# Two layers of RWKV, attention and experts: the order of the splits in the expert loop

## The chip, the cores and the metric

One core of a Trainium2 chip runs the whole program in one launch. The metric is the device time of an execution, in microseconds (us). Three executions of the kernel before took 2056.88, 2056.96 and 2059.65 us; the median is 2056.96.

## What is computed

The input is 16 sequences of 256 tokens of width 256, so 4096 tokens. Four sublayers follow each other, each with its residual and a layer norm: an RWKV attention, a quantized feed-forward net, a latent attention with 16 heads, and a mixture of 32 experts with a shared expert. Only the last one is touched:

```python
C = int(math.ceil(CF * T / E))
...
Xp = x[slots_token].reshape(E, C, d)
G = jnp.einsum('ecd,edi->eci', Xp, W_gate)
U = jnp.einsum('ecd,edi->eci', Xp, W_up)
Y = jnp.einsum('eci,eid->ecd', jax.nn.silu(G) * U, W_down)
Yf = Y.reshape(EC, d) * slots_w[:, None]
out = jnp.zeros((T, d), x.dtype).at[slots_token].add(Yf)
shared = jax.nn.silu(x @ shared_gate.T) * (x @ shared_up.T) @ shared_down.T
return (out + shared).reshape(b, s, d)
```

Each of the 32 experts has 160 slots (tokens routed to it), an inner width of 128, and weights of 256x128, 256x128 and 128x256. The shared expert has an inner width of 256 and works on all tokens.

## The kernel before

The program is a chain of phases; the last is `moe_phase`, from line 2315. Earlier phases leave the tokens' rows in DRAM (`x3`), the rows of every expert's slots in DRAM (`slots`), and six of the sixteen units of 256 tokens with their shared part done. `moe_phase` does 32 experts and the shared part of the ten units that are left (`LATE`), seven of them (`INSIDE`) within the expert loop.

Every float32 product is made of three products of float32r parts. A value is split into a high part (ACT copies it with rounding) and a low part (DVE subtracts the high part from the value), and PE sums high by high, high by low and low by high. So each operand costs an operation on ACT, then one on DVE, before PE may use it.

One expert e goes through these steps:
- SP loads its weights (`load_w`, L2416, one DMA of 384 KB into a ring of seven raw buffers) and its slots' rows (`load_slots`, L2423, into a ring of eight).
- ACT and DVE split the weights: `weights_high(e)` L2533, 128x768, and `weights_low(e)` L2646. The parts lie in a ring of three (`WRING`).
- PE transposes the rows into one PSUM bank (`expert_turn`, L2799), ACT and DVE split them: `rows_high(e)` L2540, 128x320, and `rows_low(e)` L2651. The bank is single, so the turn of the next expert waits for `rows_low`.
- PE makes the gate and up products (`expert_in`, L2813, six matmuls each), for which it waits for `rows_low(e)` and `weights_low(e)`, and for the banks to be read.
- ACT applies silu (`expert_gate`, L2548), DVE multiplies (`expert_hidden`, L2660), ACT and DVE split the product (`hidden_high` L2554, `hidden_low` L2665).
- PE makes y (`expert_out`, L2824), which waits for `hidden_low(e)` and for the copy of the y before; ACT copies y with the slots' weights (`copy_y`, L2562, two operations).
- POOL adds the rows of y into one of two DRAM arrays (`add_rows`, L2475, two indirect DMAs with accumulation; expert e uses array e % 2). It waits for the copy and, since both write the same array, for the adds of expert e-2 to have landed.

SP's loads are tied to this: `load_w(e+7)` waits for `weights_low(e)`, and `load_slots(e+7)` waits for the turn and for the landed adds of expert e-1, as the same ring place is used by its index columns.

Each engine has its own order, written out by hand as a loop over e. `unit_of(e)` gives e // 4 and the piece e % 4: four experts go with one unit u of the shared part. In iteration e:
- PE (L2834): turn(e+2); in piece 0 the shared gate products, in piece 1 the shared up products; `expert_in(e+1)`; in piece 1 the turn of the next unit's tokens, in piece 2 the shared down products; `expert_out(e)`.
- ACT (L2574): `copy_y(e-1)`; in piece 2 `x_high(u+1)` L2512; `weights_high(e+2)`; `rows_high(e+2)`; `expert_gate(e+1)`; in piece 0 the shared gate L2519, in piece 1 the shared high part L2526; `hidden_high(e+1)`.
- DVE (L2676): in piece 0 `add_shared(u-1)` L2641, in piece 2 `shared_low(u)` L2635; `weights_low(e+2)`; in piece 1 `shared_hidden(u)` L2630; `rows_low(e+2)`; in piece 2 `x_low(u+1)` L2622; `expert_hidden(e+1)`; `hidden_low(e+1)`.

After the loop PE, ACT and DVE do the shared part of the last three units. SP waits for all adds and then loads the two arrays unit by unit (`load_sums`, L2453). DVE (`combine`, L2707 and L2711) and POOL (`add_first`, L2489) add them to the units' totals, and layer norm and the store of the result follow. On DVE `combine` of the first unit (p = 0) stands ahead of the last unit's `shared_hidden`.

Of the kernel before, what the change touches and what calls it, by code (L numbers as in the profile page):

```python
# [525 lines left out]
E = 32  # L526
# [1785 lines left out]
INSIDE = 7  # L2312


def moe_phase(nc, w_experts, x3, slots_dram, sums_dram, out, ident, q_rows, wq_high, raw_kept):
    with ExitStack() as ctx:
# [77 lines left out]
        def unit_of(e):  # L2394

            return e // PACE, e % PACE
# [110 lines left out]
        def _(act):  # L2507
            def x_high(u):
                act.wait_ge(transposed, u + 1)
                if u >= 2:  # L2510
                    act.wait_ge(up_ready, u - 1)
                nc.scalar.activation(xt_part[0][:, u % 2, :, :], xt_ps[:, :].rearrange("p (k t) -> p k t", k=KD),  # L2512
                                     ACT.Copy).then_inc(xt_high, 1)
# [14 lines left out]
            def weights_high(e):  # L2528
                if e >= EARLY_RAW:
                    act.wait_ge(raw_in[e % WRAW], 16 * (e // WRAW + (0 if e % WRAW < EARLY_RAW else 1)))  # L2530
                if e >= WRING:
                    act.wait_ge(y_ready, e - WRING + 1)
                nc.scalar.activation(w_part[0][:, e % WRING, :], kept_raw(q_rows, raw_kept, e), ACT.Copy)\  # L2533
                    .then_inc(w_high, 1)

            def rows_high(e):
                act.wait_ge(e_turned, e + 1)
                if e >= 2:
                    act.wait_ge(e_up_ready, e - 1)
                nc.scalar.activation(e_part[0][:, e % 2, :, :],  # L2540
                                     et_ps[:, 0:KD * CAP].rearrange("p (k c) -> p k c", c=CAP), ACT.Copy)\
                    .then_inc(e_high, 1)

            def expert_gate(e):
                act.wait_ge(e_gate_ready, e + 1)
                if e >= 2:
                    act.wait_ge(e_hidden_done, e - 1)
                nc.scalar.activation(e_gate[:, e % 2, :], egate_ps[:, 0:CAP], ACT.Silu).then_inc(e_gate_done, 1)  # L2548
# [25 lines left out]
            for e in range(E):  # L2574
                u, piece = unit_of(e)
                if e == 0:
                    copy_y(0)
                if e >= 2:
                    copy_y(e - 1)
                if piece == 2 and u < INSIDE:  # L2580
                    x_high(u + 1)
                if e + 2 < E:
                    weights_high(e + 2)
                    rows_high(e + 2)
                if e + 1 < E:
                    expert_gate(e + 1)
                if piece == 0 and u < INSIDE:
                    shared_gate(u)
                if piece == 1 and u < INSIDE:
                    shared_high(u)  # L2590
                if e + 1 < E:
                    hidden_high(e + 1)
# [26 lines left out]
        def _(dve):  # L2619
# [55 lines left out]

            for e in range(E):  # L2676
                u, piece = unit_of(e)
                if piece == 0 and 0 <= u - 1 < INSIDE:
                    add_shared(u - 1)
                if piece == 2 and u < INSIDE:  # L2680
                    shared_low(u)
                if e + 2 < E:
                    weights_low(e + 2)
                if piece == 1 and u < INSIDE:
                    shared_hidden(u)
                if e + 2 < E:
                    rows_low(e + 2)
                if piece == 2 and u < INSIDE:
                    x_low(u + 1)
                if e + 1 < E:  # L2690
                    expert_hidden(e + 1)
                    hidden_low(e + 1)


# [288 lines left out]
```

## Time and profile before

| | us |
|---|---|
| median of three runs | 2056.96 |
| the profiled execution's own time | 2057.99 |
| its span, first to last instruction | 2055.7 |
| PE busy with matmuls | 1912.7 |
| DVE busy | 1559.1 |
| ACT busy | 1050.9 |
| POOL busy | 835.3 |
| mean granted TensorE clock, as a share of 2.4 GHz | 0.970 |

The expert loop takes about 131 us of this, from 1866 to 1997 us after the first instruction; the last three units' shared part ends near 2018, the rest is the sums and the layer norm.

In a row of a timeline the first number is the start, the second the length, both in us; then come engine, line, operation, what is written and read, and the count of instructions merged into the row. The bracket gives the idle time of the engine before it and who ended it; a row without a bracket had no idle time that counts. SPq rows are the issue of DMAs. In a row of windows there are: the stretch and its length, then each engine's busy time with its count of instructions, the granted clock, the busy share of the DMA engines and their GB/s.

### The profile page before, as it was taken

What the parts mean: (1) busy time and instruction counts of PE and PEld (TensorE: products, weight loads), DVE (VectorE), ACT (ScalarE), POOL (GpSimd) and SP (SyncE); (2) the same over time, 40 slices, a digit from 0 to 9 for tenths busy, and PEclk for the clock granted to TensorE, in tenths of its full rate; (3) what the DMA queues carried; (4) which work ended last, traced back from release to release, by engine and by line L of the source; (5) the groups of instructions that cost most, each with busy time, mean ns of one, the idle gap of its engine ahead of it and who ended that gap; (6) DMA issues with size and microseconds to landing.
All of it is one profiled execution on the core that took longest, in us unless ns stands there. A gap on an engine that the chain in (4) does not pass through costs nothing. (4 is left out here: it accounts for less than half of the span.)

```text
span 2055.7 us, 36824 instructions
## 1 busy us (share of the span) xinstructions
PE 1912.7 (93%) x12560; PEld 1717.1 (84%) x12560; DVE 1559.1 (76%) x4280; ACT 1050.9 (51%) x2677; POOL 835.3 (41%) x865
## 2 busy tenths in 40 slices
PE   7999999999999969999799999999999999977991
PEld 6788888888888858888599999999999999977881
DVE  8978878777787655565478888888888888864656
ACT  5434333333433333332377666666666666634663
POOL 1232323232232310000234466666666566744675
PEclk9999999999999979999899999999999999998995
DMA  3200000010100222743000010000000000126867
GB/s 123 83 1 32 21 11 32 1 32 1 32 21 1 75 77 90 251 150 124 19 12 17 22 38 24 20 21 19 19 18 19 18 18 13 38 77 171 193 134 247
DMA packets 101928, 118.82 MB, mean 58 GB/s; under 512 B 12551, under 2 KB 93643, under 8 KB 101104
## 3 DMA queue, kind: packets, MB, share of 16 engines
q1 hardware_dynamic: 84672, 104.16, 15.8%
q0 software_dynamic: 12288, 8.11, 2.7%
q10 hardware_dynamic: 4784, 4.21, 0.6%
q8 instruction: 102, 1.67, 0.3%
q14 instruction: 82, 0.67, 0.1%
HBM read 75.43 MB, written 57.10 MB: 64 GB/s over the span
## 5 line engine op out<-in xcount | busy, mean ns | idle before, releaser
L237 POOL TENSOR_TENSOR rwkv_gate<-rwkv_key,rwkv_gate 128x512 f32<-128x512 f32 x128 | 203.9, 1593 | 525.3 <-DVE rwkv_key L442 525.3
L1419 POOL TENSOR_TENSOR kept_raw<-kept_raw,mla_row_inv 128x512 f32<-128x512 f32 x192 | 199.3, 1038 | 302.5 <-DVE mla_row_inv L1771 301.1
L310 ACT ACTIVATE rwkv_gate<-rwkv_r 128x512 f32<-128x512 f32 x128 | 76.6, 598 | 400.7 <-DVE rwkv_o_low L363 398.1
L1576 ACT ACTIVATE kept_raw<-kept_raw,mla_least 128x256 f32<-128x256 f32 (+1 forms) x512 | 227.8, 446 | 90.9 <-DVE mla_least L1755 89.8
L1755 DVE CUSTOM_DVE_ANT_0 kept_raw<-mla_score,kept_mask 128x256 f32<-128x256 f32 (+1 forms) x512 | 156.8, 352 | 79.6 <-PE mla_score L2130 79.1
L427 DVE TENSOR_TENSOR rwkv_kv<-rwkv_v,rwkv_key 128x512 f32<-128x512 f32 x128 | 88.0, 688 | 125.2 <-PE rwkv_v L475 123.0
L434 DVE TENSOR_TENSOR_SCAN rwkv_state<-rwkv_decay_w,rwkv_kv 128x256 f32<-128x256 f32 x256 | 166.1, 691 | 4.1
L2130 PE MATMUL mla_score<-mla_k_high,mla_q_high 128*128 128x256 f32 (+1 forms) x512 | 155.3, 303 | 0.0
L492 PE MATMUL rwkv_out<-rwkv_w_high,rwkv_o_high 128*128 128x256 f32 x512 | 143.9, 281 | 5.8 <-DVE rwkv_o_low L363 5.8
L492 PE MATMUL rwkv_out<-rwkv_w_high,rwkv_o_low 128*128 128x256 f32 x512 | 145.2, 284 | 0.0
L492 PE MATMUL rwkv_out<-rwkv_w_low,rwkv_o_high 128*128 128x256 f32 x512 | 144.1, 281 | 0.0
L2130 PE MATMUL mla_score<-mla_k_high,mla_q_low 128*128 128x256 f32 (+1 forms) x512 | 143.4, 280 | 0.0
L2130 PE MATMUL mla_score<-mla_k_low,mla_q_high 128*128 128x256 f32 (+1 forms) x512 | 143.1, 279 | 0.0
L1504 POOL DMA_INDIRECT slots<-mla_x_out,mla_slot_now x128 | 129.5, 1012 | 31.6 <-issue 24.7
L1592 ACT ACTIVATE mla_p_high<-mla_turn 128x512 fp32r<-128x512 f32 x192 | 113.9, 593 | 47.8 <-PE mla_turn L2139 47.4
L1765 DVE TENSOR_TENSOR mla_p_low<-mla_turn,mla_p_high 128x512 fp32r<-128x512 f32 x192 | 127.9, 666 | 0.5 <-ACT mla_p_high L1592 0.5
L2139 PE MATMUL mla_turn<-kept_ident,kept_raw 128*128 128x128 f32 x768 | 116.1, 274 | 11.8 <-DVE mla_p_low L1765 11.8
L2139 PEld LDWEIGHTS mla_turn<-kept_ident,kept_raw 128*128 128x128 f32 x768 | 91.0, 140 | 35.7 <-issue 23.0
L2158 PE MATMUL mla_o<-mla_p_high,mla_v_high 128*128 128x256 f32 x384 | 117.0, 305 | 0.6 <-DVE mla_o_low L1776 0.4
L2475 POOL DMA_INDIRECT sums<-moe_y_rows,moe_e_rows x64 | 92.2, 1441 | 50.2 <-ACT moe_y_rows L2562 29.8
L1538 ACT ACTIVATE mla_q_high<-mla_turn 128x512 fp32r<-128x512 f32 x128 | 76.4, 599 | 66.8 <-PE mla_turn L2107 66.6
L2158 PE MATMUL mla_o<-mla_p_high,mla_v_low 128*128 128x256 f32 x384 | 107.9, 281 | 0.0
(403 smaller groups left out, 6418.7 us busy)
## 6 DMA issues: line engine op xcount, KB each, us to landing
kept_raw<-in_experts SPq DMA_DIRECT2D x27, 384.0 KB
kept_raw<-in_rkvo SPq DMA_DIRECT2D x16, 512.0 KB
moe_y_in<-sums SPq DMA_DIRECT2D x32, 256.0 KB, 5.1
sums<-ffn_empty SPq DMA_DIRECT2D x12, 512.0 KB
slots<-ffn_empty SPq DMA_DIRECT2D x16, 361.2 KB
moe_e_rows<-slots SPq DMA_DIRECT2D x32, 180.6 KB
kept_x_in<-x SPq DMA_DIRECT2D x18, 256.0 KB, 2.7
mla_x_res<-x SPq DMA_DIRECT2D x17, 256.0 KB
```

Source lines behind the costliest of these rows:

```text
L237: nc.gpsimd.tensor_tensor(gate[:, c % 2, :], key[:, c % 2, :], gate[:, c % 2, :], ALU.mult).then_inc(gated_done, 1)
L434: last_scan = nc.vector.tensor_tensor_scan(out=state[:, q, 1:SEQ + 1], data0=decay_w[:, c:c + 1].to_broadcast([P, SEQ]), data1=kv[:, q * S ...
L492: last = nc.tensor.matmul(out_ps[j // 2][:, (j % 2) * D:(j % 2 + 1) * D], o_part[op][:, c % 2, j * P:(j + 1) * P], w_part[wp][:, c, 3 * D: ...
L1419: nc.gpsimd.tensor_tensor(unit, unit, row_inv[:, v % PR, 0:len(heads)].rearrange("p (h a) -> p h a", a=1) .to_broadcast([P, len(heads), ke ...
L1504: nc.gpsimd.indirect_dma_start(slots_dram, bass.IndirectOffsetOnAxis(slot_now[:, of % 2, i:i + 1], 0), x_out[:, of % 2, i // TOPK, :], Non ...
L1576: last = nc.scalar.activation(probs[:, v % PR, i * keys:(i + 1) * keys], masked[:, v % 2, i * keys:(i + 1) * keys], ACT.Exp, bias=least[:, ...
L1592: nc.scalar.activation(p_part[0][:, v % PR, :], turn_ps[n % TURN_BANKS][:, :], ACT.Copy)\
L1755: last = nc.vector.tensor_tensor_reduce(out=masked[:, v % 2, i * keys:(i + 1) * keys], in0=score_ps[v % 2][:, i * keys:(i + 1) * keys], in ...
L1765: nc.vector.tensor_tensor(p_part[1][:, v % PR, :], turn_ps[n % TURN_BANKS][:, :], p_part[0][:, v % PR, :].bitcast(F32), ALU.subtract).then ...
L2130: last = nc.tensor.matmul(score_ps[v % 2][:, i * keys:(i + 1) * keys], q_part[qp][:, tile, h * P:(h + 1) * P], k_part[kp][:, par, 0:keys], ...
L2139: last = nc.tensor.transpose(ps[:, i * P:(i + 1) * P], probs[:, v % PR, i * P:(i + 1) * P], ident[:, :])
L2158: last = nc.tensor.matmul(out, v_part[vp][:, seq % 2, kb, b, :], probs_t, start=(i == 0), stop=(i == len(terms) - 1))
```

## The change

ACT and DVE keep their instructions and waits; their order inside an iteration changes. The high and low parts of expert e+2's rows go ahead of those of its weights. In pieces 0 and 1 of the seven units inside the loop (`busy`) the weights follow directly. In pieces 2 and 3, and for the experts behind the last inside unit, `weights_high(e+2)` goes behind `expert_gate(e+1)`, and `weights_low(e+2)` goes between `expert_hidden(e+1)` and `hidden_low(e+1)`. PE, POOL and SP are as they were.

```diff
@@ -2579,11 +2579,15 @@
                     copy_y(e - 1)
                 if piece == 2 and u < INSIDE:
                     x_high(u + 1)
+                busy = piece < 2 and u < INSIDE
                 if e + 2 < E:
-                    weights_high(e + 2)
                     rows_high(e + 2)
+                    if busy:
+                        weights_high(e + 2)
                 if e + 1 < E:
                     expert_gate(e + 1)
+                if e + 2 < E and not busy:
+                    weights_high(e + 2)
                 if piece == 0 and u < INSIDE:
                     shared_gate(u)
                 if piece == 1 and u < INSIDE:
@@ -2675,20 +2679,24 @@
 
             for e in range(E):
                 u, piece = unit_of(e)
+                busy = piece < 2 and u < INSIDE
                 if piece == 0 and 0 <= u - 1 < INSIDE:
                     add_shared(u - 1)
                 if piece == 2 and u < INSIDE:
                     shared_low(u)
                 if e + 2 < E:
-                    weights_low(e + 2)
+                    rows_low(e + 2)
+                    if busy:
+                        weights_low(e + 2)
                 if piece == 1 and u < INSIDE:
                     shared_hidden(u)
-                if e + 2 < E:
-                    rows_low(e + 2)
                 if piece == 2 and u < INSIDE:
                     x_low(u + 1)
                 if e + 1 < E:
                     expert_hidden(e + 1)
+                if e + 2 < E and not busy:
+                    weights_low(e + 2)
+                if e + 1 < E:
                     hidden_low(e + 1)
```

## Rows read from the trace of the kernel before

**Rows 1.** Timeline of PE, pieces 2 and 3 of a unit and two first turns

```profile
1949.79 0.43 PE L2813 MATMUL moe_egate<-moe_e_high,moe_w_high 128*128 128x160 f32 x2
...
1951.44 0.32 PE L2824 MATMUL moe_y<-moe_w_high,moe_eh_high 128*80 128x256 f32 x1
...
1953.61 0.47 PE L2799 MATMUL moe_et<-kept_ident,moe_e_rows 80*128 80x80 f32 x4 [1.26 <-DVE moe_e_low L2651]
...
1985.38 0.47 PE L2799 MATMUL moe_et<-kept_ident,moe_e_rows 80*128 80x80 f32 x4 [1.27 <-DVE moe_e_low L2651]
```

**Rows 2.** Timeline of ACT in pieces 2 and 3 of the unit before 1953.61

```profile
1946.66 0.59 ACT L2512 ACTIVATE moe_xt_high<-moe_xt 128x512 fp32r<-128x512 f32 x1
1947.14 0.85 ACT L2533 ACTIVATE moe_w_high<-kept_raw 128x768 fp32r<-128x768 f32 x1
1947.87 0.43 ACT L2540 ACTIVATE moe_e_high<-moe_et 128x320 fp32r<-128x320 f32 x1
...
1950.24 0.34 ACT L2554 ACTIVATE moe_eh_high<-moe_e_hidden 128x160 fp32r<-128x160 f32 x1 [1.74 <-issue]
1950.48 0.82 ACT L2562 ACTIVATE moe_y_rows<-moe_y,moe_e_rows 80x256 f32<-80x256 f32 x2
1951.19 0.84 ACT L2533 ACTIVATE moe_w_high<-kept_q_rows 128x768 fp32r<-128x768 f32 x1
```

**Rows 3.** Timeline of DVE in the same two pieces

```profile
1948.02 0.96 DVE L2646 TENSOR_TENSOR moe_w_low<-kept_raw,moe_w_high 128x768 fp32r<-128x768 f32 x1 [1.18 <-ACT moe_w_high L2533]
1948.89 0.48 DVE L2651 TENSOR_TENSOR moe_e_low<-moe_et,moe_e_high 128x320 fp32r<-128x320 f32 x1
1949.29 0.68 DVE L2622 TENSOR_TENSOR moe_xt_low<-moe_xt,moe_xt_high 128x512 fp32r<-128x512 f32 x1
1949.89 0.32 DVE L2660 TENSOR_TENSOR moe_e_hidden<-moe_eup,moe_e_gate 128x160 f32<-128x160 f32 x1
...
1952.99 0.48 DVE L2651 TENSOR_TENSOR moe_e_low<-moe_et,moe_e_high 128x320 fp32r<-128x320 f32 x1
```

**Rows 4.** Timelines of PE, ACT, DVE in piece 0, input products and their readers

```profile
1955.39 0.36 PE L2813 MATMUL moe_egate<-moe_e_high,moe_w_high 128*128 128x160 f32 x2
...
1956.22 0.30 ACT L2548 ACTIVATE moe_e_gate<-moe_egate 128x160 f32<-128x160 f32 x1 [0.38 <-PE moe_egate L2813]
...
1956.89 0.32 DVE L2660 TENSOR_TENSOR moe_e_hidden<-moe_eup,moe_e_gate 128x160 f32<-128x160 f32 x1
```

**Rows 5.** Windows of the core by unit, and of experts 28 to 31

```profile
1904.40:1921.80 17.40, 16.04 (x128) 15.65 (x128) 10.26 (x21) 11.27 (x27) 11.21 (x8) 0.90 0.82 186
1953.60:1969.50 15.90, 14.53 (x129) 14.15 (x129) 10.19 (x21) 11.27 (x27) 11.77 (x8) 1.00 0.89 215
1985.40:1997.30 11.90, 10.89 (x69) 10.40 (x70) 5.64 (x13) 7.13 (x19) 8.87 (x7) 0.71 0.41 44
```

**Rows 6.** Timeline of POOL: first issues of adds 4, 10, 12, 22, 24; last issue

```profile
1894.15 1.40 POOL L2475 DMA_INDIRECT sums<-moe_y_rows,moe_e_rows  x1 [0.55 <-issue]
...
1920.30 1.40 POOL L2475 DMA_INDIRECT sums<-moe_y_rows,moe_e_rows  x1 [1.42 <-ACT moe_y_rows L2562]
...
1927.74 1.92 POOL L2475 DMA_INDIRECT sums<-moe_y_rows,moe_e_rows  x1 [0.85 <-DMA sums<-moe_y_rows,moe_e_rows]
...
1967.96 1.40 POOL L2475 DMA_INDIRECT sums<-moe_y_rows,moe_e_rows  x1 [1.40 <-ACT moe_y_rows L2562]
...
1976.18 1.40 POOL L2475 DMA_INDIRECT sums<-moe_y_rows,moe_e_rows  x1 [1.62 <-DMA sums<-moe_y_rows,moe_e_rows]
...
2003.65 1.40 POOL L2475 DMA_INDIRECT sums<-moe_y_rows,moe_e_rows  x1 [0.30 <-issue]
```

**Rows 7.** Timeline of SP: a slots load released by an add; the sums' loads

```profile
1975.40 0.32 SPq L2423 DMA_DIRECT2D moe_e_rows<-slots  x1
...
2006.90 27.05 SPq L2453 DMA_DIRECT2D moe_y_in<-sums  x32
```

**Rows 8.** Timeline of DVE behind the loop: the first sums are combined

```profile
2010.99 0.68 DVE L2711 TENSOR_TENSOR kept_q_rows<-moe_y_in 128x512 f32<-128x512 f32 x1
```

## The prediction, written before the changed kernel was run

> **What bounds the kernel now.** I read first the chain of waits over the expert loop, then each engine's timeline over one unit of it, then the windows by unit, and last POOL's and SP's timelines, because their work outlives the loop. The change touches only this loop, from about 1866 to 1997 us.
>
> A unit is four experts, pieces 0 to 3. The first turn of a unit on PE (`expert_turn`, piece 0) starts at 1953.61 and, two units later, at 1985.38 [rows 1]: 15.88 us a unit. I count us from a unit's first turn, and the unit that ends at 1953.61 begins at 1937.73. What is to be seen in [rows 1] is the hole: PE stands idle 1.26 and 1.27 us before these turns, waiting for L2651, `rows_low`; and before the y products at 1951.44 (13.71) it loses another 0.35, the expert's input products having begun at 12.06 and taking 1.30. PE's work without holes is 14.1 us a unit; the rest, 1.8, is wait.
>
> The cause stands in [rows 2, 3]. In piece 2, ACT goes `x_high` 8.93, `weights_high` 9.41, `rows_high` 10.14, then the gate, then 1.74 us of nothing until `hidden_high` at 12.51, because DVE runs `weights_low` 10.29, `rows_low` 11.16, `x_low` 11.56 and only then `expert_hidden` 12.16. So the next copy of y starts at 12.75, piece 3's weights and rows follow it, and `rows_low` ends 0.14 us before the late turn. The two big operations on the weights, 0.84 us on ACT and 0.96 on DVE, stand ahead of a short chain that PE waits for.
>
> **The change, part by part.** Nothing is added or removed: same instructions, same waits, same DMAs. Moved are ACT's and DVE's weights parts, and with them the semaphore that SP's `load_w` and PE's `expert_in` wait for. From start to start ACT takes 0.48 for `x_high`, 0.73 for `weights_high`, 0.32 for `rows_high`, 0.71 for a copy of y, 0.2 for a gate; DVE takes 0.87 for `weights_low`, 0.40 for `rows_low`, 0.60 for `x_low`; 0.03 us lie between the two, 0.35 between `expert_hidden` and `hidden_high`, and 0.14 before PE [rows 2, 3]. From the first input product, the gate is ready after 0.83 us and the up half after 1.50 [rows 4].
>
> Pieces 0 and 1: rows before weights only exchanges neighbours. `weights_low` ends 0.1 to 0.3 us later, and PE's next input products come over an us after it. In piece 1 the shared hidden part falls behind it, so ACT enters piece 2 about 0.25 us later: that I charge.
>
> Piece 2: `x_high` 9.18, `rows_high` 9.66, gate 9.98, `weights_high` 10.18 to 11.02; DVE `rows_low` 10.12, `x_low` 10.52, `expert_hidden` 11.12 (12.16 before), `weights_low` 11.36 to 12.32 (it ended at 11.25), `hidden_low` 12.24 to 12.57. Piece 3: the input products need that `weights_low`, so they start at 12.46 instead of 12.06: **a new wait of 0.40 us on PE**. The copy of y starts at 12.01, when y is there; the y products follow the input products without a gap, 13.76 to 14.48; `rows_low` is done at 13.68, so the next unit's turn starts at 14.48. Next `weights_low` ends at 15.32, 0.84 after that turn, while `expert_in` is preceded by 1.5 us of shared products: covered. Behind the moved `weights_low` on DVE stands `hidden_low`, for which PE's y products wait; it ends over a us before they can start. Saved: 15.88 − 14.48 = **1.40 us at each of seven boundaries, 9.8**.
>
> Experts 28 to 31 have no shared product to cover the moved `weights_low`, and there PE's granted clock is 0.71 in the mean [rows 5]. At the full clock I work out 10.9 us instead of 11.9 for this stretch; at half clock throughout, with the new waits, 12.6. From +1.0 to −0.7: I take 0, for the row lies between the two levels.
>
> The unit from 1904.4 took 17.40 us with a granted clock of 0.90; an undisturbed one has 15.9 and 1.00 [rows 5]. This fall cost 1.5 us and came behind a 1.3 us hole. Between keeping and losing it I take that it goes, since the hole does: +1.5. PE, ACT and DVE would thus be through with the loop 11.3 us earlier.
>
> **What then is late next: the adds.** POOL adds each expert's y into one of two DRAM arrays, and an add waits until that of two experts before has landed. It is nearly the bound already: add 12 starts 7.44 us after add 10 and add 24 starts 8.22 after add 22, each released by a DMA; the start comes 0.78 after the landing that SP sees at 1975.40 [rows 6, 7]. Issues of 1.40 with 0.30 between set a floor of 3.4 per expert. The new pace asks for 14.48 / 2 = 7.24 us per two experts; the chain gives 7.44 to 8.22. I take 7.8, the middle, since early and late pairs are as many. Add 4 starts at 1894.15 now, about 0.9 earlier after the change; ten such pairs later add 24 starts at 1971.2 instead of 1976.18. By then the loads are over and adds go at 3.41 (before there was a wait for ACT among them): the last add takes 3.1 for its two issues and lands 1.8 after the second, as now (2003.65 + 1.40 to 2006.90). That is 7 × 3.41 + 3.1 + 1.8 = 28.8 us later, at 2000.0 instead of 2006.90 [rows 6, 7]: 6.9 us. SP may load the sums only then. `combine(0)` on DVE, at 2010.99, stands ahead of the last unit's `shared_hidden`, and nothing idles before it [rows 8]: the sums have some slack there, between 0 and 1.4 us, of which I take half. So the end moves by the smaller of 11.3 and 6.9 + 0.7: **7.6 us**.
>
> The slots of expert e+7 are loaded when add e−1 has landed, so the slots come nearer to their turn on PE as the adds fall behind the loop. SP's loads run five turns ahead, so I cost this at nothing; if it did stop PE, the sums would be late by as much anyway.
>
> The sum stands against the profiled execution, span 2055.7, time 2057.99; the median of the runs is 2056.96, 1.03 below, and the saving is taken from the median: 2049.4.
>
> **Rivals.** (1) *The adds keep up.* For it: the earlier pair of 7.44 is nearly fast enough, and then the loop's own 11.3 us decides: 2045.7. Against: the late pair, 8.22.
>
> (2) *The adds keep their old pace* to add 24, and the gain is only what lies behind: 30.7 − 28.8 = 1.9, with slack 0.7 about 2.6: 2054.4. For it: the DMA engines are 0.89 busy over a unit [rows 5]; squeezed into 14.48 us that is 0.98, so landings can grow by what the loop saves, and with them the slots. Against: the loads wait for the adds and can't crowd them more than now. The Trainium skill, "DMA: Bandwidth & Descriptors", section "Issuing engines are not separate DMA queues", says that transfers issued by different engines run on the same 16 engines and interleave. By that rule alone the adds' landings grow with the loads' density, which is this rival and its 2054.4, in place of a pace of 7.8.
>
> (3) *Slower: TensorE's clock falls oftener.* Place: the new 0.40 us wait in each piece 3, and experts 28 to 31. A fall like that of the 1904.4 unit costs 1.5; one twice as long 3.1. It decides from seven short falls on; with twice as long falls in five of seven units the loop is 15.5 − 9.8 = 5.7 longer: 2062.7. Against: PE waits less per unit, and holes of 0.35 us were never followed by a fall in the undisturbed units. The Trainium skill, "TensorE: Matmul & The Clock Gate", section "Loop structure matters more than you think", says that products that follow each other immediately keep the clock up. By that the change raises the clock, and the 1.5 us are rightly counted as gained.
>
> (4) *No effect*: the hole at the boundary turns out to be set by something I misplaced, for instance by `weights_low` after `expert_hidden` costing all that rows ahead of it gain: 2057, within a us or two.
>
> **Numbers.** Chances: my forecast (savings of 4.1 to 10 us) 0.55, rival 1 0.20, rival 2 0.15, rival 3 0.04, rival 4 0.06. What can be told from no change is 0.2%, 4.1 us. Faster: 0.55 + 0.20 = 0.75 and a little of rival 2, 0.77; slower 0.04; same 0.19. The range takes in forecast and rival 1 with the clock's and experts 28 to 31's bound, 2056.96 − 12.3 = 2044.7, and reaches rival 2 at its upper end: 2054.6.
>
> **What would show it.** Unit period 14.5 us on PE; the 1.26 us hole gone and one of 0.4 before piece 3's L2813, released by DVE `weights_low`; ACT's 1.74 us wait about halved. POOL's waits for its own DMA grow from 0.8 to several us in all and its last add starts about 7 us earlier; DVE L2711 now idles before p = 0, waiting for `y_in`. Wrong if the period stays above 15.5, if PE waits for slots, or if L2711 doesn't wait although the loop gained over 9.

## The result: 4.0 us faster, and the profile after

| | kernel before, same chip | changed kernel |
|---|---|---|
| median (lowest to highest), us | 2058.18 (2054.68 to 2060.51), 12 runs | 2054.20 (2051.49 to 2057.76), 12 runs |
| ratio, 95% interval | | 0.9981 (0.9973 to 0.9989) |
| profiled execution: time, span, us | 2057.99, 2055.7 | 2051.49, 2049.3 |

The change saves 4.0 us, where 7.6 were forecast. The two profiled executions lie 6.4 us apart in their spans, but the one of after is the lowest of its twelve, and its first add starts 1.64 us earlier than before, at 1873.29 instead of 1874.93. In both it starts 9.56 us after the loop's first turn on PE, so this difference comes from stages that the change does not touch. I count therefore from the first add to the end: 180.8 us before, 176.0 after.

The loop itself. First the windows of the core for three consecutive units after, each from first turn to first turn (start and end, then us, busy us and instructions of PE, PEld, DVE, ACT and POOL, the granted clock, the DMA engines' share, GB/s):

```profile
1885.94:1900.22 14.28, 14.28 (x131) 14.19 (x130) 10.25 (x21) 11.36 (x28) 11.04 (x8) 1.00 0.82 184
1900.22:1914.49 14.27, 14.27 (x131) 14.16 (x130) 10.24 (x21) 11.36 (x28) 9.70 (x7) 1.00 0.81 197
1914.49:1928.76 14.27, 14.27 (x130) 14.18 (x129) 10.13 (x20) 11.30 (x28) 11.17 (x9) 1.00 0.88 201
```

PE is busy in all of each unit, 14.27 or 14.28 us at a granted clock of 1.00, where [rows 5] had 15.90 and 17.40. The timeline of PE after, over pieces 2 and 3 of the second of these units, shows where the hole was:

```profile
1900.22 0.44 PE L2807 MATMUL moe_et<-kept_ident,moe_e_rows 80*128 80x80 f32 x4
...
1911.98 0.44 PE L2807 MATMUL moe_et<-kept_ident,moe_e_rows 80*128 80x80 f32 x4
1912.40 0.42 PE L2821 MATMUL moe_egate<-moe_e_high,moe_w_high 128*128 128x160 f32 x2
...
1913.78 0.28 PE L2832 MATMUL moe_y<-moe_w_high,moe_eh_high 128*80 128x256 f32 x1
...
1914.49 0.44 PE L2807 MATMUL moe_et<-kept_ident,moe_e_rows 80*128 80x80 f32 x4
```

From first turn to first turn it is 14.27 us, piece 3's input products start 12.18 after the first, directly behind the turn before them, and the next first turn has no wait before it: compare [rows 1]. ACT and DVE in the same pieces, from their timelines after:

```profile
1909.66 0.43 ACT L2540 ACTIVATE moe_e_high<-moe_et 128x320 fp32r<-128x320 f32 x1
1909.97 0.30 ACT L2548 ACTIVATE moe_e_gate<-moe_egate 128x160 f32<-128x160 f32 x1
1910.16 0.86 ACT L2533 ACTIVATE moe_w_high<-kept_raw 128x768 fp32r<-128x768 f32 x1
1911.47 0.34 ACT L2554 ACTIVATE moe_eh_high<-moe_e_hidden 128x160 fp32r<-128x160 f32 x1 [0.46 <-DVE moe_e_hidden L2664]
```

```profile
1910.12 0.49 DVE L2655 TENSOR_TENSOR moe_e_low<-moe_et,moe_e_high 128x320 fp32r<-128x320 f32 x1 [0.60 <-ACT moe_e_high L2540]
1910.52 0.68 DVE L2626 TENSOR_TENSOR moe_xt_low<-moe_xt,moe_xt_high 128x512 fp32r<-128x512 f32 x1
1911.12 0.32 DVE L2664 TENSOR_TENSOR moe_e_hidden<-moe_eup,moe_e_gate 128x160 f32<-128x160 f32 x1
1911.35 0.95 DVE L2650 TENSOR_TENSOR moe_w_low<-kept_raw,moe_w_high 128x768 fp32r<-128x768 f32 x1
```

In us from 1900.22, `expert_hidden` (L2664) starts at 10.90, where [rows 3] had 12.16 and the prediction 11.12; the 1.74 us in which ACT waited [rows 2] are 0.46. The last three units, from 1928.76 on, are longer, 14.84, 14.54 and 15.43 us: PE waits for slots, 0.39 us before the turn at 1943.60 and 0.97 before that at 1973.57.

So PE, ACT and DVE are through early, and something else sets the end. The timeline of POOL after (as in [rows 6]: the first issues of adds 4, 22 and 24, and the last issue of all):

```profile
1893.12 1.40 POOL L2475 DMA_INDIRECT sums<-moe_y_rows,moe_e_rows  x1 [1.12 <-DMA sums<-moe_y_rows,moe_e_rows]
...
1963.88 1.40 POOL L2475 DMA_INDIRECT sums<-moe_y_rows,moe_e_rows  x1 [1.39 <-DMA sums<-moe_y_rows,moe_e_rows]
...
1971.31 1.40 POOL L2475 DMA_INDIRECT sums<-moe_y_rows,moe_e_rows  x1 [0.89 <-ACT moe_y_rows L2562]
...
1997.15 1.40 POOL L2475 DMA_INDIRECT sums<-moe_y_rows,moe_e_rows  x1 [0.31 <-issue]
```

The bracket before add 24, at 1971.31, names ACT's copy of y. But ACT's timeline has this copy ended at 1962.94, 8.37 us earlier. An add has one other wait, for the landing of the add two experts before, so that is what held it:

```profile
1962.11 0.83 ACT L2562 ACTIVATE moe_y_rows<-moe_y,moe_e_rows 80x256 f32<-80x256 f32 x2
```

SP's load of the sums:

```profile
2000.46 27.07 SPq L2453 DMA_DIRECT2D moe_y_in<-sums  x32
```

[rows 7] had it at 2006.90. And what waits for those sums, on DVE and on PE behind it:

```profile
2004.10 0.69 DVE L2719 TENSOR_TENSOR kept_q_rows<-moe_y_in 128x512 f32<-128x512 f32 x1 [6.20 <-DMA moe_y_in<-sums]
```

```profile
2007.61 0.80 PE L2795 MATMUL moe_down_ps<-kept_wq_high,moe_h_high 128*128 128x256 f32 x2 [9.01 <-DVE moe_h_low L2639]
```

DVE stands 6.20 us before `combine(0)`, where [rows 8] had no wait, and PE 9.01 behind it. The loop's gain is there, standing still. Page section 4, the chain that ended last, says the same. Of before, its longest groups were PE's y products and ACT's `weights_high`, with 1% of the span each. Its line by group now begins:

```profile
DMA sums<-moe_y_rows,moe_e_rows 2%; POOL sums L2475 2%; DVE moe_stats L2723 0%; ACT moe_x_out L2612 0%; PE moe_egate L2821 0%; PE moe_eup L2821 0%; PE moe_y L2832 0%; DVE moe_total L2715 0%; PE moe_gate_ps L2776 0%; DVE moe_var_eps L2735 0%; PE moe_et L2807 0%; PE moe_down_ps L2795 0%; PE moe_up_ps L2776 0%; DVE moe_moments L2732 0%; DMA moe_e_rows<-slots 0%
```

### The profile page after: what moved, and what is told of

It is laid out like the page before. It is cut to its first block and busy times, and to the rows that moved or that the text cites. A ratio compares the mean times of both kernels' runs of the same rounds, so it can differ in the third digit from the quotient of the medians.

```text
span 2049.3 us, 36824 instructions
## 1 busy us (share of the span) xinstructions
PE 1906.0 (93%) x12560; PEld 1711.6 (84%) x12560; DVE 1560.3 (76%) x4280; ACT 1052.6 (51%) x2677; POOL 835.8 (41%) x865
## 5 line engine op out<-in xcount | busy, mean ns | idle before, releaser
L1592 ACT ACTIVATE mla_p_high<-mla_turn 128x512 fp32r<-128x512 f32 x192 | 113.9, 593 | 48.6 <-PE mla_turn L2139 48.4
```

## Experiments

Times are medians, with the ratio to the kernel before on the same chip in the same job and its 95% interval. "Adds 4 to 24" is from start to start on POOL; "landing" is from the end of an add's second issue to the start of the slots load that waits for it on SP, as a mean over the 12 even and the 12 odd experts from 0 to 23. Where SP came to that load after the landing, this gives an upper bound: the waits view counts 14 to 21 waits of SP for adds in the kernels before and changed, so not all of the 24 are exact. Phases are of one profiled execution each.

| us | first add starts | adds 0 to 4 | 4 to 24 | 24 to sums' loads | sums' loads to end | landing, even and odd |
|---|---|---|---|---|---|---|
| before | 1874.93 | 19.22 | 82.03 | 30.72 | 48.8 | 3.3, 2.7 |
| b_again | 1876.37 | 19.07 | 83.05 | 30.50 | 48.5 | 3.6, 2.4 |
| after | 1873.29 | 19.83 | 78.19 | 29.15 | 48.8 | 3.9, 2.2 |
| a_again | 1874.50 | 18.10 | 81.31 | 30.57 | 48.6 | 3.4, 2.9 |
| a_third | 1876.08 | 18.94 | 81.08 | 30.98 | 48.8 | 3.7, 2.9 |
| a_four | 1874.40 | 18.37 | 71.36 | 30.04 | 48.7 | 4.5, 2.7 |
| a_light | 1873.67 | 18.67 | 73.47 | 30.71 | 48.9 | 2.6, 2.8 |

How far an add runs behind the loop is read from two timelines, the end of its copy on ACT and the start of its first issue on POOL. With the old order the add starts 0.8 to 1.1 us after the copy, for every add from 0 to 23, in before, b_again and b_four: the loop set the adds' pace. In after this distance grows to 4.8 us at add 8 and 8.4 at add 24, in a_again and a_third to 6.1 and 9.6 at add 24. An add that starts over 1 us after its copy was not held by the copy. Counted so, POOL's waits of 0.4 us or more before adds 5 to 24 are:

| us | behind a copy | behind a landing |
|---|---|---|
| before | 12.0 | 3.3 |
| b_again | 15.7 | 1.1 |
| after | 0 | 10.9 |
| a_again | 0 | 10.7 |
| a_third | 0 | 9.6 |
| a_four | 0 | 0 |

### The changed kernel again, and with half of the adds

The two kernels named half, one of each order, issue and await only the first of the two DMAs of each add:

```diff
-                for a in range(2):
+                for a in range(1):
                     nc.gpsimd.indirect_dma_start(
                         sums_dram[e % SUMS],
```

The same stands in the four loops that wait for `y_added`. The other half of an expert's rows of y is never added to the sums. The first kernel is the changed one, unaltered.

> The changed kernel once more, for the spread between executions. Theory A (the adds bound the end): the unit period on PE is again 14.5 us, POOL runs almost without idle time from add 19 on, the sums' loads start within 2 us of 2000.5, and what differs between this profiled time and the 2051.5 of the first profile is found in falls of TensorE's clock outside the expert loop, in stages that the change does not touch. Rival B (the gain inside the loop is itself unsteady): units of 15.5 us or more, or waits of PE for slots of several us, appear. Ratio to the kernel before between 0.9972 and 0.9990.

> The kernel before with only the first of the two indirect DMAs of each add (half of every expert's rows is not added). Theory A: in the old order the loop's pace was ACT's and DVE's, so it stays at 15.9 us a unit; only the tail gains, as the sums come up to 4 us earlier than the slack uses: 0 to 3 us less than before. Rival B (the adds do not matter in either order): the same time as before within 0.5 us.

> The changed kernel with only the first of the two indirect DMAs of each add (half of the rows is not added). Theory A (the end is set by the adds, and the loop's own gain is bigger than what was measured): the difference to the old order with halved adds is the loop's full gain, 9 to 12 us, and the span is 2038 to 2041 us. Rival B: the difference to the old order with halved adds is the same 4 to 6 us as with whole adds.

Measured: a_again 2056.84 against 2059.06, ratio 0.9989 (0.9980 to 0.9998); b_half 2056.84, 0.9992 (0.9982 to 1.0002); a_half 2045.81, 0.9936 (0.9924 to 0.9948). With half of the adds the old order gains 2.2 us, within the noise, and the new one is 2056.84 − 2045.81 = **11.0 us** faster than the old one; from the two intervals I estimate 3 us of uncertainty either way. That is what reaches the end of the kernel when the adds do not hold it back. From the loop's first turn to the end of its last copy of y it is 132.9 and 133.4 us in before and b_again, and 119.6 in a_half, where the last six of the seven units take 14.27 or 14.28 us. With all adds a_again keeps 2.2 of it, the first job's kernel 4.0.

What held a_again back, by the waits view of 1862 to 2000 us (who waits for whom: us in total, times, longest), one window of it, and one row of PE's timeline:

```profile
POOL sums L2475 <- DMA sums<-moe_y_rows,moe_e_rows: 9.6, 12, 1.5
...
PE moe_et L2807 <- DMA moe_e_rows<-slots: 7.8, 3, 5.8
```

```profile
1949.90:1959.00 9.10, 9.10 (x55) 9.10 (x54) 4.40 (x9) 4.95 (x11) 7.28 (x5) 0.62 0.87 205
```

```profile
1949.41 0.50 PE L2807 MATMUL moe_et<-kept_ident,moe_e_rows 80*128 80x80 f32 x4 [1.79 <-DMA moe_e_rows<-slots]
```

The 5.8 us stand at the loop's start; the other two waits, 2.0 us, are late slots within it. (The first row counts only the waits that the view puts down to a landing.) The longer one, 1.79 us before the turn at 1949.41 (third fence), was directly followed by 9.1 us at a granted clock of 0.62: PE's two levels, mostly the lower. A late add thus comes back as a late slot, and that, once in three profiles of the changed kernel, as a fall of the clock. The Trainium skill, "TensorE: Matmul & The Clock Gate", section "Loop structure matters more than you think", says that products which follow each other immediately keep the clock up; the three units of 14.27 and 14.28 us above, without a hole and at 1.00, agree. They don't prove it, as the unit of before from 1953.60 has the hole and 1.00 too [rows 5].

### Only the rows ahead, the weights never inside the chain

```diff
-                busy = piece < 2 and u < INSIDE
+                busy = True
```

This stands in ACT's and DVE's streams, so that `weights_high` and `weights_low` follow the rows directly in all pieces.

> The changed kernel with the rows' parts ahead of the weights' in every expert, but the weights' parts directly behind them everywhere (never inside the expert's own chain). By the hand schedule the unit period is about 14.7 us instead of 14.5, because hidden_high is late by the weights' 0.9 us only in piece 2. Theory A: 0.2 us a unit are hidden behind the adds, so the time is that of the changed kernel within 1 us. Rival C (it is the weights' place inside the chain that brings the gain): half or more of the gain is lost, time 2056 or more where the kernel before takes 2058.

Measured: 2056.52 against 2059.06, 0.9987 (0.9979 to 0.9996), the same as a_again's 2056.84 beside it. The time came as theory A had it, the loop did not. PE's timeline has two first turns of units 15.48 us apart, where 14.7 were expected:

```profile
1904.21 0.47 PE L2807 MATMUL moe_et<-kept_ident,moe_e_rows 80*128 80x80 f32 x4
...
1919.69 0.47 PE L2807 MATMUL moe_et<-kept_ident,moe_e_rows 80*128 80x80 f32 x4
```

The last six of the seven units take 15.47 to 15.51. So of the 1.6 us that an undisturbed unit loses by the change, the rows ahead bring 0.4 and the weights inside the chain 1.2. In the whole kernel these 1.2 us a unit are worth nothing that shows: at add 24 the adds are 3.5 us behind their copies here, and 6.1 to 9.6 in the changed kernel, where the faster loop only runs further ahead of them.

### Slots two experts later

```diff
-                if e >= 1 and e - 1 + RING < E:
-                    load_slots(e - 1 + RING)
+                if e >= 3 and e - 3 + RING < E:
+                    load_slots(e - 3 + RING)
```

> The changed kernel with SP's slots loads two experts later in SP's order: load_w(e+7) then load_slots(e+5), which waits for the adds of expert e-3 instead of e-1. The loads' bytes are the same, but they are no longer released in bursts by each landing. Theory A (the adds' chain sets the end, and its landings are long because each releases 565 KB of loads ahead of the next): the landings' mean falls from 3.1 us to 2.5 or less, adds 4 to 24 take 72 to 75 us instead of 78 to 81, the time is 3 to 6 us below the changed kernel. Rival D (POOL's issue and a fixed landing time set the pace, whoever loads): no change within 1 us.

> The kernel before with the same later slots loads. Theory A with the old order: PE's loop at 15.9 us a unit becomes the only bound inside the loop, adds follow it as before; gain 0 to 1.5 us, from the last adds alone. Rival E (the adds were already the bound of the old kernel, and the order of the parts is worth little by itself): a gain as large as for the changed kernel, 3 us or more.

Measured: a_spread 2055.69 against 2059.24, 0.9984 (0.9975 to 0.9993); b_spread 2059.68, 1.0004 (0.9995 to 1.0013). No change that can be told from the kernels they were made of. SP, the queue that issues the loads, still waited 67.4 us for adds in a_spread, against 77.0, 69.8 and 63.2 in the three profiles of the changed kernel, so the release of a load by a landing was not undone, and adds 4 to 24 took 79.2 us where theory A had 72 to 75. The run says nothing for or against that theory.

### The tail: the last unit's hidden part ahead of the first sums

```diff
                 for p in range(first, first + units):
-                    combine(g, p)
                     if p == 0:
                         shared_hidden(LATE - 1)
                         shared_low(LATE - 1)
+                    combine(g, p)
```

> The changed kernel with the last unit's shared_hidden and shared_low on DVE ahead of combine of p = 0 (with the old place, they wait for the sums). If combine of p = 0 is what the sums hold up, as PE's 9 us wait for L2639 shows, the last shared products are done while the sums are on their way, DVE has 2 us less behind them, and the time falls by 0.5 to 1.5 us. If the end is paced by the sums' DMAs and POOL's first additions alone: no change within 0.5 us.

> The changed kernel with both: slots loads two experts later and the last shared part ahead of combine. Theory A: the gains add, 4 to 7 us below the changed kernel, about 0.3% below it and 0.4 to 0.5% below the kernel before. Rival D: nothing but what the second edit brings, at most 1.5 us.

Measured: a_tail 2054.89 against 2059.24, 0.9981 (0.9971 to 0.9991); a_both, which is a_tail with the slots two experts later, 2053.79, 0.9973 (0.9961 to 0.9985). From the sums' loads to the end it takes 47.9 and 47.4 us instead of 48.5 to 48.8. So PE's 9.01 us behind `combine(0)` are worth about an us: the sums' loads, 27 us of issue on SP, are the longer part of the tail.

### How far executions differ

> The kernel before once more, one profile, to see how far two executions of the same kernel differ. Theory A: from the first add to the sums' loads 130.5 to 132.5 us (131.97 in the first profile), and from these loads to the end 48.7, the same as for the changed kernel: the sums set the tail in the old kernel too. The first add starts anywhere from 1873 to 1877 us, by what TensorE's clock did in the earlier stages.

> The changed kernel, a third profile. Theory A: from the first add to the sums' loads 127 to 130 us, and 48.7 from there to the end; the two profiles so far have 127.2 and 130.0. If a third lies outside, the pace of the adds varies more than was seen.

Measured: one execution each, 2059.67 for the kernel before and 2058.11 for the changed one. Their rows in the table, beside those of before, after and a_again, show how much of the first pair's difference was luck. In mean over two and three executions, the change takes adds 4 to 24 from 82.5 to 80.2 and the whole from the first add to the end from 181.0 to 178.1, thus 2.8 us and not 4.8. The start of the first add varies by 3.1 us among these five and by 4.9 among all the kernels here, 1873.3 to 1878.2. In these five it comes 9.50 to 9.56 us after the loop's first turn on PE, so nearly all of this stems from work that none of them touches.

### Adds that don't wait for each other

```diff
+        spare = [nc.dram_tensor(f"spare{a}", (SUMROWS, D), F32).ap() for a in range(2)]
...
-                if e >= SUMS:
+                if e >= 4:
                     for a in range(2):
-                        pool.wait_ge(y_added[(e - SUMS) % RING][a], 16 * ((e - SUMS) // RING + 1))
+                        pool.wait_ge(y_added[(e - 4) % RING][a], 16 * ((e - 4) // RING + 1))
...
-                        sums_dram[e % SUMS],
+                        (sums_dram + spare)[e % 4],
```

The experts' rows go to four arrays in turn, and two of these are read by nobody: half of the experts are missing from the sums. All DMAs are issued, with the same bytes. The kernel named light is another way to the same end: it loads 128 of the 768 columns of the weights of experts 7 to 31, which then compute with what lay in the buffers, and its adds wait as ever.

```diff
+                cols = EW if e < WRAW else P
-                sp.dma_start(kept_raw(q_rows, raw_kept, e), w_experts[e]).then_inc(raw_in[e % WRAW], 16)
+                sp.dma_start(kept_raw(q_rows, raw_kept, e)[:, 0:cols], w_experts[e][:, 0:cols])\
+                    .then_inc(raw_in[e % WRAW], 16)
```

> The changed kernel with the adds going to four arrays in turn, two of them read by nobody (so half of the experts' rows is missing in the result), and each add waiting for the one of four experts before instead of two: same DMAs, same loads, without the wait on the landing. Theory A1 (the wait for the landing of two experts before is what holds the adds): POOL never waits for a DMA, adds 4 to 24 take 72 to 74 us instead of 78 to 81, the time is 3 to 6 us below the changed kernel. Theory A2 (POOL's own issuing, 3.4 us an expert, and late starts hold them): at most 2 us below.

> The changed kernel with the weights of experts 7 to 31 loaded in their first 128 of 768 columns only (the rest are an earlier expert's), 8 MB less of loads. Theory A3 (the landings are long because loads crowd the same DMA engines): landings of 2 us in the mean instead of 3.1, adds 4 to 24 in 72 to 74 us, 3 to 6 us below the changed kernel. Theory D (a landing takes its 3 us whatever else is loaded): within 1.5 us of the changed kernel.

> The kernel before with four arrays in turn and each add waiting for that of four experts before (half of the experts' rows is missing in the result). It completes the square: with the changed order this edit brought about 9 us. Theory A (in the old order the loop's own pace, 15.9 us a unit, is the bound, and the adds' wait only in the changed order): 0 to 2.5 us below the kernel before, adds 4 to 24 take 79.5 to 82 us. Rival E (the adds bound the old kernel as well, by the same wait): 5 us or more below.

Measured: a_four 2047.32 against 2058.19, 0.9946 (0.9925 to 0.9966); a_light 2047.39, 0.9952 (0.9937 to 0.9966); b_four, the old order with the same edit as a_four, 2058.20 against 2058.37, 0.9997 (0.9988 to 1.0006). The gain of a_four and a_light is larger than the 3 to 6 us below the changed kernel that were expected.

These give a square. Old order with the adds' wait and without it: no difference. New order with it: 2.2 to 4.0 us. New order without it: **10.9 us** (7.0 to 15.4 by the interval). The wait of one add for the one two experts before cost nothing in the old order and costs 7 to 9 us in the new one. POOL's waits in a_four, by the waits view:

```profile
POOL sums L2477 <- ACT moe_y_rows L2564: 16.7, 3, 12.1
POOL sums L2477 <- issue: 8.8, 29, 0.3
POOL spare L2477 <- issue: 7.6, 25, 0.3
...
POOL spare L2477 <- ACT moe_y_rows L2564: 2.1, 7, 0.3
```

There is no wait for a DMA, and adds 4 to 24 take 71.36 us, 7.14 per two experts. That is the loop's own pace, since its units are 14.26 to 14.28 us here, and up to add 24 each add starts 0.8 to 2.2 us behind its copy. That the landings in this run are longer than anywhere (4.5 and 2.7), while it is among the two fastest kernels, shows that a long landing costs nothing by itself; only the wait for it does. In b_four they are 4.3 and 2.3, also longer than in before, with the same loads at the same pace: the density of the loads is not all that lengthens them. The edit also spreads the rows over four arrays instead of two; as the landings are longer in it and not shorter, the gain does not come from quicker landings. In a_light landings are short instead, and POOL hardly waits:

```profile
POOL sums L2477 <- DMA sums<-moe_y_rows,moe_e_rows: 2.5, 4, 0.9
```

So the load of weights beside the even landings has a part in their length: with a sixth of its bytes they fall from 3.4 to 3.9 us (the three profiles of the changed kernel) to 2.6 in this one profile. Light loads were not tried in the old order, so of a_light's gain it stays open whether all of it came by way of the adds.

### Slots four experts later, and the queue that they stand in

```diff
-                if e >= 1 and e - 1 + RING < E:
-                    load_slots(e - 1 + RING)
+                if e >= 5 and e - 5 + RING < E:
+                    load_slots(e - 5 + RING)
```

> The changed kernel with SP's slots loads far enough back in SP's order, load_w(e+7) then load_slots(e+3), that they wait for adds four experts older than now; with two experts SP still waited 67 us for the adds. Theory A (a landing that releases loads at once makes the next one long): SP's waits for adds fall below 30 us, landings even out near 3 us, adds 4 to 24 take 74 to 79 us, and the time is 1 to 4 us below the changed kernel. Rival F (the loads' amount counts, not their moment): same within 1 us, or slower if PE waits for slots that come later.

> The same, and the last unit's shared_hidden and shared_low ahead of combine of p = 0. From the sums' loads to the end 47.4 to 47.9 us instead of 48.7, as in the two runs that had this edit; so about 1 us below the run with the later slots loads alone, whatever that one gives.

Measured: a_back5 2082.34 against 2058.37, 1.0111 (1.0095 to 1.0127); a_back5_tail, the same with the tail's edit, 2080.04, 1.0107 (1.0091 to 1.0122). **24 us slower**, a miss. The waits view of SP over 1862 to 2010 us in a_back5 and, in the second fence, PE's beside it:

```profile
SPq L2411 <- DVE moe_total L2645: 66.1, 6, 12.9
SPq L2416 <- DVE moe_w_low L2650: 31.9, 9, 5.8
SPq L2422 <- DMA sums<-moe_y_rows,moe_e_rows: 4.8, 2, 3.5
```

```profile
PE moe_et L2807 <- DMA moe_e_rows<-slots: 28.0, 7, 7.2
```

The wait for adds is gone from SP, as meant: 4.8 us where it was 77.0. But SP is one queue in order. `load_x` of a later unit, which waits until `add_shared` (L2645) has freed its buffer, was until then reached late, because SP had been held at the slots; now SP comes to it up to 12.9 us early, and the next slots stand behind it. The wait that ends at 1908.40 below was released by the `add_shared` that DVE ran from 1907.69 to 1908.37. SP's timeline:

```profile
1895.11 0.38 SPq L2423 DMA_DIRECT2D moe_e_rows<-slots  x1
1908.40 0.38 SPq L2411 DMA_DIRECT2D moe_x_rows<-x  x1
1908.83 1.13 SPq L2416 DMA_DIRECT2D kept_raw<-in_experts  x1
1910.06 0.37 SPq L2423 DMA_DIRECT2D moe_e_rows<-slots  x1
```

Fifteen us lie between two loads of slots that PE wants every 3.6 us, and PE's turn at 1915.43 waited 4.90 for its slots. The remedy is to ask for x one unit later as well:

```diff
-                if piece == 0 and u >= 1 and u - 1 + XRING < LATE:
-                    load_x(u - 1 + XRING)
+                if piece == 0 and u >= 2 and u - 2 + XRING < LATE:
+                    load_x(u - 2 + XRING)
```

> As the run with load_slots(e+3) behind load_w(e+7), but with load_x one unit later in SP's order, since there SP stood 66 us at load_x for a total of the shared part and the slots behind it came late. If that was the whole of the 22 us, PE no longer waits for slots beyond the 4.7 us at the start. Theory A (a landing that releases loads at once makes the next one long): adds 4 to 24 take 74 to 79 us and the time is 1 to 4 us below the changed kernel. Rival F (the amount of the loads counts, not their moment): within 1 us of it.

> The same, and the last shared part ahead of combine of p = 0: from the sums' loads to the end about 1 us less than 48.7. Theory A: 2 to 5 us below the changed kernel, the fastest of all that compute the whole result; rival F: 1 us below.

Measured: a_back5x 2055.05 against 2060.33, 0.9972 (0.9962 to 0.9983); a_back5x_tail 2053.58, 0.9971 (0.9960 to 0.9982). The 24 us are gone, so they were that place in the queue. SP's waits in a_back5x:

```profile
SPq L2422 <- DMA sums<-moe_y_rows,moe_e_rows: 30.6, 14, 5.4
```

They are less than half of the 63.2 to 77.0 in the changed kernel, but adds 4 to 24 take 78.35 us, as in the best profile of the changed kernel, and POOL waits 9.5 us for its own DMAs. Theory A's 74 to 79 us takes in both, so it is not shown. With the tail's edit the sums' loads to the end are 47.7 us instead of 49.2. Ratios of 0.9971 and 0.9972 are the lowest of kernels that compute everything, with a_both's 0.9973; their intervals overlap with that of the changed kernel, 0.9973 to 0.9989, so by how much they beat it is not settled.

## Why the prediction was right about the loop and half wrong about the time

**The bound of the kernel before** was right: the hole before each first turn, made by the weights' parts ahead of a short chain. b_four adds what the profile alone couldn't say, that in the old order the adds' wait bound nothing; the adds there start 0.8 to 1.1 us behind their copies.

**The loop, 11.3 us.** Right in the mechanism and near in the size: 11.0 reach the end by a_half against b_half, 10.9 by a_four. Piece 3's input products were put at 12.46 and its next first turn at 14.48; in an undisturbed unit they came at 12.18 and 14.27. The new wait of 0.40 us on PE did not come, and ACT was not 0.25 us later in piece 2: `expert_hidden` and with it `weights_low` came 0.22 us before the forecast, and PE reached the input products as the weights were ready. The loop left to itself is through 13 to 14 us earlier, 119.6 us instead of 132.9 and 133.4, so 11.3 was somewhat small. With the real adds it is 121.4, 124.4 and 124.3: late slots hold PE, and in a_again the clock falls. The unit's fall of the clock went too in the first profile: three units in a row at 1.00. In a_again one came back, 9.1 us at 0.62, behind a wait for slots that the prediction had costed at nothing. Experts 28 to 31 ran at 1.00 in all three profiles of the changed kernel, where [rows 5] had 0.71; with the adds as the bound, that didn't reach the end.

**What is late next.** Right: the adds, then the sums' loads, then `combine(0)` with DVE and PE standing.

**The adds' pace, 7.8 us per two experts: the step that failed.** It was taken as the middle between pairs of 7.44 and 8.22 [rows 6]. Adds 12 and 24 were indeed held by a landing, and so was add 20, 7.40 after add 18; all others ran at the loop's pace and said nothing of the chain's own. So the term stood on two pairs of a loop less dense. In the first profile of the changed kernel it was 78.19 / 10 = 7.8, in a_again and a_third 8.1; the mean is 8.0. The reason shows in the held adds: from the end of the second issue of add e−2 to the first issue of add e it was 4.3, 4.3 and 5.1 us in before, and 4.7, 5.0 and 5.4 in the means of after, a_again and a_third. The old order has 8.25 in the mean of its two profiles, which is the pace of a loop with units of 15.9 us and some of 17.4. So this term is 82.5 − 80.2 = 2.3 us, not 4.0, the largest of the misses.

**The start of add 4, 0.9 us.** From the first add on it is 0.2: 19.15 in the mean of before, 18.96 after.

**From add 24 to the sums' loads, 28.8 instead of 30.7.** Measured 29.15, 30.57 and 30.98, a gain of 0.4 in the mean instead of 1.9. The first of these went nearly as worked out. In a_again add 25 waited 1.36 us at 1978.38. Its copy had ended at 1972.07, so it was held by the landing of add 23, and an issue behind it took 1.99 us instead of 1.40. In a_third add 25 waited 0.93 us and its first issue took 2.12. The prediction had the adds at 3.41 us each from add 24 on, without a wait.

**The slack of 0.7.** Nothing. The first combination did come 3.64 us after the sums' loads began instead of 4.09, but from those loads to the end it is 48.8 before and after.

The sum by these is 0.2 + 2.3 + 0.4 + 0 = 2.9 us in place of 7.5, and the medians say 4.0 and 2.2. The bound was named rightly; each of its four terms was put too high, the pace by 1.7 us and the way behind add 24 by 1.5.

**The rivals.** Rival 1, that the adds keep up, was wrong with the real adds and right within half a us without their wait: 10.9 to 11.0 against 11.3. Rival 2, that they keep their old pace, at 2.6 us, lies nearest to what was measured, 2.2 to 4.0. That is in part luck: the old pace of 8.2 was the loop's, and the new one of 8.0 is that of the landings. Its reason, landings that grow with the density of the loads, fits but is not settled: the mean of all 24 landings is 3.0 us in both profiles of the old order, 3.1, 3.1 and 3.3 in those of the new and 2.7 in a_light, but 3.3 in b_four too, where the loop was as slow as before. The Trainium skill, "DMA: Bandwidth & Descriptors", section "Issuing engines are not separate DMA queues", says that transfers from different engines share the same DMA engines and interleave; a_light's even landings agree, 2.6 us instead of 3.4 to 3.9. I gave this rival too little. The argument against it, that the loads wait for the adds and can't crowd them more, did not hold: the held adds waited longer, 4.7 to 5.4 us instead of 4.3 to 5.1. It may be that a landing, by releasing a load at once, lengthens the next one; a_spread and a_back5x were to test that and left it open. Rival 3 was wrong as priced: no falls behind the new order's own waits. Rival 4 was wrong.

**The signs.** The period came at 14.3 instead of 14.5; the end of the hole, a shorter wait of ACT (0.46, under half of 1.74) and DVE's wait at `combine(0)` came as said. The wait of 0.40 before piece 3's input products did not come. POOL's waits for its own DMAs grew, from 3.3 and 1.1 us to 10.9, 10.7 and 9.6 before adds 5 to 24; the waits view alone hides this in the first profile, with 5.2 before and 4.0 after, since it puts some waits down to copies long done. The last issue came 6.5 us earlier, 1.64 of it by earlier stages, and PE did wait for slots, 2.0 us within the loop after and 4.5 in a_third, which the prediction had named as a sign against it.

What stays open: what makes a landing long besides the loads, and why long and short ones alternate. The array is not the reason, since in a_again the even landings are the long ones up to expert 14 and the odd ones from expert 15 on.

## What to carry to other kernels

When a loop is shortened, ask first whether the chain that becomes the next bound ever ran squeezed. Here each add started 0.8 us after its copy, so the old pace was the loop's; only three pairs showed the chain's own, and a forecast from so few wants a wide range. When a wait is put down to an engine, compare its time with the end of that engine's work: a copy that ended 8.37 us before holds nobody. A kernel with the chain's wait removed, in both orders, tells in two runs whether the gain was lost there: here nothing in the one order and 7 to 9 us in the other. Before one load is moved back in an in-order queue, read what else that queue will now come to early.

## What the runs showed of the hardware

The last add of all landed 1.91 us after its issue (1998.55 to 2000.46), when nothing was being loaded any more. Within the loop landings run from 1.8 to 4.9 us in the profile of after and up to 5.9 in a_four, and there they alternate from one expert to the next: 4.86, 1.92, 3.90, 1.82, 4.73, 2.87 for experts 0 to 5. With less than half of SP's waits for adds, a_back5x had its adds no faster than the best profile of the changed kernel. An issue of an add, 1.40 us on POOL with 0.30 before the next, was at times longer, up to 2.18 in before and 2.12 in a_third. Moving one load back by four experts in SP's queue cost 24 us, more than twice what all of the loop's holes had cost. And one wait of 1.79 us on PE was followed by 9.1 us at a granted clock of 0.62, and the hole of 1.27 before 1904.42 in before by 4.78 us at 0.64, while the same hole before 1953.61 and waits of 0.97, 0.62 and, in a_third, 1.73 us cost only themselves.
